# A fifth token tile for the gathered path of a product-key expert layer, and one tile fewer in the third dense chunk

## The reference

```python
q = (x @ Wq).reshape(b, t, H, 2, DK)                    # H = 4 heads
s1, i1 = top_k(sim1, 8); s2, i2 = top_k(sim2, 8)        # of 128 keys each
final_scores, pk_idx = top_k(s1[..., :, None] + s2[..., None, :], 8)
w_down = e_down[final_indices]; w_up = e_up[final_indices]
hidden = silu(einsum('btd,bthkd->bthk', x, w_down)) * relu(final_scores)
out = einsum('bthk,bthkd->btd', hidden, w_up)
x = x + tanh(g_ffn[3]) * out
```

## Time and profile before

| | us |
|---|---|
| median of 3 runs (1953.71 to 1954.48) | 1954.18 |
| the profiled execution's own time | 1956.58 |
| its span, first to last instruction | 1954.8 |
| busy: PE 1430.2, DVE 1471.8, ACT 903.4, POOL 485.4 | |
| `retrieve_phase`, from its first load | about 705 |
| chunk 0, chunk 1, chunk 2 of the dense path | 213.2, 217.3, 195.3 |

### The profile page before, as it was taken

The page is one execution under the profiler, slowest core; times in us unless marked ns, Lnnn a source line. Parts: engine busy times, 40 slices in busy tenths (PEclk is TensorE's granted clock), DMA queues, the critical chain, the costliest instruction groups (busy, mean ns, idle before and its releaser), DMA issues. The chain is left out here.

```text
span 1954.8 us, 24549 instructions
## 1 busy us (share of the span) xinstructions
PE 1430.2 (73%) x6624; PEld 1049.0 (54%) x6624; DVE 1471.8 (75%) x3100; ACT 903.4 (46%) x1768; POOL 485.4 (25%) x483
## 2 busy tenths in 40 slices
PE   4899048868999407444562488079999899999998
PEld 2455014436777203233431387068888778877776
DVE  7999479972555598699669599696777778886775
ACT  3464446643333141154321122138888688873343
POOL 0000012220000041423104022402455355545530
PEclk8999579988999755665695699599999999999999
DMA  4010400001000210145200100304666676667753
GB/s 161 22 33 1 177 6 1 0 18 47 1 0 0 92 50 1 43 156 171 71 1 10 49 22 22 104 9 145 182 202 206 180 209 204 204 195 218 215 173 113
DMA packets 82130, 181.51 MB, mean 93 GB/s; under 512 B 13832, under 2 KB 23176, under 8 KB 81168
## 3 DMA queue, kind: packets, MB, share of 16 engines
q0 software_dynamic: 27120, 91.25, 16.5%
q1 hardware_dynamic: 54944, 89.56, 13.9%
HBM read 165.04 MB, written 15.73 MB: 92 GB/s over the span
## 5 line engine op out<-in xcount | busy, mean ns | idle before, releaser
L2117 POOL DMA_INDIRECT L3f_gd<-rows,idx x128 | 151.2, 1181 | 309.2 <-DVE L3f_gd L2336 301.3
L2182 PE MATMUL L3f_o_ps<-L3f_euh,L3f_ath 128*128 128x512 f32 x384 | 158.4, 413 | 15.3 <-DVE L3f_atl L2317 14.6
L2170 PE MATMUL L3f_h_ps<-L3f_xh,L3f_edh 128*128 128x512 f32 x384 | 151.0, 393 | 7.9 <-DVE L3f_xl L2322 7.9
L2155 PE MATMUL L3f_g_ps<-L3f_oh 128*128 128x128 f32 x768 | 106.5, 283 | 62.1 <-DVE L3f_oh L2305 62.1
L2182 PE MATMUL L3f_o_ps<-L3f_euh,L3f_atl 128*128 128x512 f32 x384 | 151.1, 394 | 0.0
L2182 PE MATMUL L3f_o_ps<-L3f_eul,L3f_ath 128*128 128x512 f32 x384 | 150.8, 393 | 0.0
L2170 PE MATMUL L3f_h_ps<-L3f_xl,L3f_edh 128*128 128x512 f32 x384 | 150.6, 392 | 0.0
L2170 PE MATMUL L3f_h_ps<-L3f_xh,L3f_edl 128*128 128x512 f32 x384 | 150.3, 391 | 0.0
L2117 POOL DMA_INDIRECT L3f_gu<-in_L_ffn_e_up,idx x128 | 128.0, 1000 | 67.5 <-issue 36.4
L2155 PEld LDWEIGHTS L3f_g_ps<-L3f_oh 128*128 128x128 f32 x768 | 100.4, 195 | 73.4 <-issue 68.2
L2313 DVE TENSOR_TENSOR L3f_at<-L3f_at,L3f_G 128x512 f32<-128x512 f32 x96 | 66.2, 690 | 96.1 <-ACT L3f_at L2219 81.7
(11 more groups left out here) (509 smaller groups left out, 3681.7 us busy)
## 6 DMA issues: line engine op xcount, KB each, us to landing
L3f_eu<-in_L_ffn_e_up SPq DMA_DIRECT2D x96, 256.0 KB
L3f_ed<-in_L_ffn_e_down SPq DMA_DIRECT2D x96, 256.0 KB
L2x_ed<-in_L_ffn_e_down POOLq DMA_DIRECT2D x32, 256.0 KB, 3.8
rows<-L2x_eo POOLq DMA_DIRECT2D x32, 256.0 KB, 2.6
ternary_wgu<-in_L_ffn_w_gate_upT SPq DMA_DIRECT2D x4, 1408.0 KB, 8.8
X<-in_x SPq DMA_DIRECT2D x4, 1024.0 KB, 10.3
L0x_V<-in_ctxT SPq DMA_DIRECT2D x8, 512.0 KB, 3.9
L1f_C<-in_ctx SPq DMA_DIRECT2D x2, 2048.0 KB
```

The costliest lines, as they stand in the source:

```text
L2117: pool.indirect_dma_start(buf[j % ND][:, :], None, table, bass.IndirectOffsetOnAxis(ap=idx[:, j:j + 1], axis=0)).then_inc(sem[j % ND], 16)
L2155: last = pe.matmul(g_ps[h][:, g, :], lhsT=oh2[h][:, g, :], rhs=oh1[h][:, g, :], start=True, stop=True)
L2170: last = pe.matmul(h_ps[h][:, :], lhsT=w[h][:, c, :], rhs=x[:, c, :], start=(c == 0 and m == 0), stop=(c == DC - 1 and m == 2))
L2182: last = pe.matmul(o_ps[a][:, :], lhsT=w[h][:, a * P:(a + 1) * P], rhs=x[h][:, :], start=False, stop=False)
```

## The change

A constant `NG` = 5 replaces the 4 gathered tiles; `TG` becomes 11, `NU` 160, and the chunks have `tiles` = 4, 4 and 3 tiles. In chunks 0 and 1 a turn takes four pairs; in chunk 2 it takes three, three, three and two, in turns of four, 44 in all. The matmuls of `hidden` in chunk 2 have 384 columns, and `add_up`, `begin` and `end` go over three tiles; `silu`, `weight`, `high`, `low` take 384 columns there. There are 88 groups to build (`NO`) and no longer 96, so building ends with turn 27, `one_hot` with turn 26. To find room, `far` is gone: `one_hot` writes its intermediate into `oh1` and works in place, and `io` and `zero` use the memory of `ident` and `identb`. The final stores are of five and of three tiles.

```diff
+NG = 5
...
-    TG, S, SG, LAG, ND = NT - 4, 32, 8, 12, 6
-    NU = 4 * S
+    TG, S, SG, LAG, ND = NT - NG, 32, 8, 12, 6
+    NU = NG * S
+    tiles = [min(4, TG - 4 * q) for q in range(NQ)]
...
+    NO = TG * P // (4 * GR)
...
-            c = 3
+            c = 4 if q < NQ - 1 else 3 - (k % 4 == 3)
             pairs_in[q, k] = range(u, min(u + c, NU + LAG))
...
-        def hidden(n):
+        def hidden(n, q):
+            cols = tiles[q] * P
...
-                        last = pe.matmul(h_ps[h][:, :], lhsT=w[h][:, c, :], rhs=x[:, c, :],
+                        last = pe.matmul(h_ps[h][:, 0:cols], lhsT=w[h][:, c, :], rhs=x[:, c, 0:cols],
...
-                for a in range(4):
+                for a in range(tiles[q]):
                     for w, x in ((ath, euh), (ath, eul), (atl, euh)):
...
         def one_hot(n, h):
...
-            if done:
-                act.wait_ge(oh1_ready, done)
             for g in range(GR):
-                act.activation(far[:, g, :], io[:, :], ACT.Abs, scale=-1.0, bias=first[:, 0, n * GR + g:n * GR + g + 1]).then_inc(far_ready, 1)
+                act.activation(oh1[h][:, g, :], io[:, :], ACT.Abs, scale=-1.0, bias=first[:, 0, n * GR + g:n * GR + g + 1]).then_inc(far_ready, 1)
...
-            build = q < NQ - 2 or q == NQ - 2 and k < NP - 1
-            if q < NQ - 1:
+            held, build = n + EB < NO, n + EB + 2 < NO
+            if held:
                 keep(n + EB, q + 1, k, 0)
...
-        for t in range(4):
-            dve.tensor_scalar(xs[:, t, :], X[:, TG + t, :], stat[:, t:t + 1], stat[:, 4 + t:5 + t],
+        for t in range(NG):
+            dve.tensor_scalar(xs[:, t, :], X[:, TG + t, :], stat[:, 0, t:t + 1], stat[:, 1, t:t + 1],
```

More of the change, by code:

```diff
@@ L1825, in route_phase @@
     E1 = A["L3_ffn_e_down"].shape[0]
-    NQ, TG = 3, NT - 4
+    NQ, TG = 3, NT - NG
     tg = R["tg"]
@@ L1890, in _, with pair @@
         pe.wait_ge(k_in, 32)
-        def pair(i, regroup):
+        def pair(i, *regroup):
             for h in range(2):
@@ L1915, in _ @@
         with pe.Fori(0, TG // 2) as i:
-            pair(i, True)
+            pair(i, True, True)
         for i in range(TG // 2, NP):
-            pair(i, False)
+            pair(i, 2 * i < TG, False)
     @block.scalar
@@ L2183, in add_up, with end @@
                 last.then_inc(used, 1)
-        def end():
-            for a in range(4):
+        def end(q):
+            for a in range(tiles[q]):
                 last = pe.matmul(o_ps[a][:, :], lhsT=zero[:, :], rhs=zero[:, 0:1].to_broadcast([P, D]), start=False, stop=True)
@@ L2195, in _ @@
             pe.wait_ge(xl_ready, DC * (q + 1))
-            hidden(q * EB)
+            hidden(q * EB, q)
             begin(q)
[L2198 to L2202, removed]
+            add_up(q * EB, q, q < NQ - 1, q > 0)
+            built = min(NP, max(1, (NO - (q + 1) * EB) // 2))
+            if built > 1:
+                with pe.Fori(1, built) as k:
+                    hidden(q * EB + 2 * k, q)
+                    add_up(q * EB + 2 * k, q, True)
+            if built < NP:
+                with pe.Fori(built, NP) as k:
+                    hidden(q * EB + 2 * k, q)
+                    add_up(q * EB + 2 * k, q, False)
+            end(q)
     @block.scalar
@@ L2363, in turn @@
                 down_low(n + 2, 0)
-            low(n, 0)
+            low(n, 0, cols)
             up_low(n + 1, 1)
@@ L2367, in turn @@
             gathered(js[:1])
-            low(n + 1, 1)
+            low(n + 1, 1, cols)
             if more:
@@ L2393, in _ @@
         for q in range(NQ):
-            dve.wait_ge(G_ready, (q + 1) * EB + 2)
+            dve.wait_ge(G_ready, min((q + 1) * EB, NO) + 2)
             for k in range(NP):
-                turn(q, k, q < NQ - 2 or q == NQ - 2 and k < NP - 1, q < NQ - 1 or k < NP - 1)
+                turn(q, k, (q + 1) * EB + 2 * k + 2 < NO, q < NQ - 1 or k < NP - 1)
             if q < NQ - 1:
```

57 lines of the change are left out of this document (29 added, 28 removed).

## The result

| | before | after |
|---|---|---|
| median, us | 1953.95 (1952.1 to 1954.48, 4 runs) | 1979.87 (1978.92 to 1984.16, 4 runs) |
| profiled execution, its span | 1956.58, 1954.8 | 1978.92, 1977.1 |
| chunk 0 | 213.1 | 231.4 |
| chunk 1 | 217.3 | 234.9 |
| chunk 2 | 195.4 | 183.4 |

The change makes the kernel slower: the ratio is 1.0136, with an interval of 1.0119 to 1.0152. Chunks 0 and 1 give away 35.9 us, chunk 2 takes back 12.0, start and tail 1.7; together that is the 22.3 us between the two spans.

What follows compares the result with a forecast made beforehand. Chunks 0 and 1 stood where PE's floor meets the `ed` load loop, chunk 2 on the `eu` loop. -19 + 27.6 - 1 + 0.5 + 1.3 = +9.4 us gave 1963.6 us; likeliest case 1958 to 1980, full range 1930 to 1984.

Steps and rivals of the forecast that it cites:

- T = 9.38 + L: Chunks 0 and 1: turn time T in us, L the second `ed` load's latency from issue to copy; at least 12.69.
- A fourth pair a turn: Chunks 0 and 1: extra gathers lengthen the awaited `ed` load to L = 4.6, +1.1 us a turn; +27.6 us in all.
- Narrower chunk: Chunk 2: 384-column matmuls cut PE's work, but the `eu` loop holds back part of the gain; -19 us.
- The clock rival: Chunk 2: PE's idle time lowers its clock, 2.7 us each fall, +16 us in six turns, 1980 us; chance 0.05.
- The first rival: Chunks 0 and 1: extra gathers do not delay the `ed` load, L near 3.5; about 1934 us, faster; chance 0.32.
- Both loops lengthen: Chunks 0 and 1: the `eu` load is delayed too, ACT waits twice a turn, T about 15; 1998 us; chance 0.05.
- The break-even: Chunks 0 and 1: the `ed` load's latency L below which the change gains, put at 3.85 us.
- cancel: Whole kernel: L near 3.9 and chunk 2 as forecast offset each other, within 4 us of 1954; chance 0.13.
- DVE's cover: Chunks 0 and 1: DVE's 1.37 us idle ahead of the next `weight` takes the fourth pair's 1.36 us for nothing.
- Fewer groups: After turn 27: building ends earlier, so PE and ACT have less work, turns about 12.7 us; -1 us.
- Chunk 1 to chunk 2: At this change of chunk DVE passes straight from its last pair to `split_x`, so the fourth pair shows; +1.3 us.
- Prelude: Before the chunks: one more `xs`; +0.5 us.

Runs made afterwards that it cites:

- e9: Changed kernel, but the fourth pair's `gd` gather (ahead of the `ed` load) fetches 128 of 512 columns, the `gu` gather whole; 1945.55 us (1 run).
- e10: Changed kernel, but the fourth pair's `gu` gather (behind the `ed` load) fetches 128 of 512 columns, the `gd` gather whole; 1968.66 us (1 run).
- e4: Changed kernel with the fourth pair moved on DVE from the turn's end to behind the second pair; 1982.48 us (4 runs), ratio 1.0154.
- e2: Changed kernel with three pairs in every turn and only 128 of its 160 pairs, the last tile's gathered part left out; 1935.43 us (1 run).
- e5: Changed kernel with two buffers each for `ed` and `eu`, and `ND` = 5; 1913.59 us (4 runs), ratio 0.9804 to the kernel before.
- e3: Changed kernel, but both gathers at the fourth place of a turn fetch 128 of 512 columns; 1947.23 us.
- e1: Kernel before, with its 4 gathered tiles, taking four pairs a turn in chunks 0 and 1 and nothing else of the change; 1989.7 us (1 run).
- e12: Changed kernel, but POOL holds back the fourth pair's two gathers until ACT has copied the next turn's second `ed` load; 1999.77 us (4 runs), ratio 1.024.
- e8: Changed kernel with two buffers for `ed`, one for `eu`, and `ND` = 5; 1929.16 us (1 run).

## Why the prediction was right or wrong

The direction was right and the loop named was the one that binds; the size was too small, 9.4 us where the profiled executions show 22.3 (medians: 25.9).

- **The form T = 9.38 + L**: right, in all 17 undisturbed turns.
- **"A fourth pair a turn", L = 4.6: the first term that failed.** The bound above was the `eu` load's 5.21, and the discount, "another load had been issued shortly ahead of it, so I stay under it", had no price in the trace: there was such a load, an `ed` issued 1.9 us ahead at 1802.37, but nothing read there said what it cost. L measured 4.98 and 5.19, so +1.4 and +1.8 a turn and not +1.1: 26 us in 17 turns, where the term had 19. e9, e10 and e4 show what should have been asked of that row: not how many gathers are near the load, but whether one was issued just before it. The `eu` load had one 1.2 us ahead, and so has the new one, at 0.5.
- **"Narrower chunk", -19: the second term that failed**; it came to -12.0. The working took 9 us off ten turns with gathers and 8 off the five behind them; the runs show 5 and 6. It did not ask what the `ed` buffer's round takes when `silu` no longer sets it: 6.3 to 6.6 us a block, 12.9 a turn where it shows; ACT's waits for `ed` stood in the trace of before, 8.9 us beside the 10.8 for `eu`. And it put the clock at nothing. e2, without the fourth pair, gets 15.0 us, so 4 of the missing 7 us are there without it; the other 3 are no more than single runs differ by. One reading of the working was off as well: the turns with gathers took not 11.8 us but 12.5 (turns 32 to 41 of before, 1754.48 to 1879.94), since 16 turns less five are 11 and not 11.7.
- **The clock rival** was given 0.05 and "in six turns it is +16". It came in part, beside the forecast: by the estimate above the lower level costs 6.3 us more in chunk 2 than before (8.0 against 1.7). The forecast said "in pieces too short for it"; single waits of up to 3.5 us for `atl`, 22.1 us in all, stood against that. The Trainium skill's warning (TensorE: Matmul & The Clock Gate, HAM oscillation), that DMA waits between bursts of matmuls send the clock down again and again, agrees with this trace, which has four falls in chunk 2 where before had one. That it is worth 6 us is estimated, and seen on the chain for one fall of 2.8 us; it was not tried alone. e5, with doubled buffers, has no fall in chunk 2, and e2 and e3, with single ones, have several.
- **The first rival** (no delay, 1934) fell by L. While the load was under way, POOL's queue moved 0.77 MB in turn 11 where it had moved 0.36. The Trainium skill's rule that each DMA engine goes round between the queue rows that have work (DMA: Bandwidth & Descriptors, Queues, rings and completion order) did not exempt the load, though it has a queue of its own. In what order the engines took the packets is not shown here. **Both loops lengthen** (1998) fell too: in chunk 0 ACT waits for no `eu` load between 1390 and 1530 us.
- **The break-even** was misread: by the forecast's own sum, which changes by 24 us for 1 us of L, +9.4 becomes 0 at L = 4.2 and not at 3.85. So "cancel" belonged at 4.2, and at 3.9 the sum has -7. L came out above either, so this changed nothing in the direction.
- **DVE's cover** of 1.37 us: right, and used up to the last tenth.
- **Fewer groups** (-1): turns 27 to 30 take 52.0 us, where they took 51.8; nothing. In e1, which builds on with four pairs, they take 57.3. **Chunk 1 to chunk 2** (+1.3): turn 31 to the end of `split_x` is 3.2 us longer. **Prelude** (+0.5) and **end** (0): -0.4 and -1.3.

Against the forecast chunks 0 and 1 are 2.4 and 4.9 us over 229 and 230, chunk 2 7.4 over 176, and the edges 2.2 below: 12.5, and with the rounding of the forecast's stages the 12.9 between 9.4 and 22.3.

## What to carry to other kernels

A buffer that is loaded again only when it has been used puts the load's whole latency into the loop; then "the DMA engines have room" says little, and what is issued just ahead of that load can be paid in each turn, as the gather 0.5 us ahead was here. Work out the round of each single buffer (issue, latency, copy, release) beside the engines' floors before filling idle time with other transfers, for the loops that bind now and for those that come next when one of them is shortened. Where such a round is within a few tenths of the floor, double the buffer first and judge the change then: here the same edit cost 26 us before and gained 22 after.

## What the runs showed that was not expected

- The order of issue counts more than the bytes near by: a 256 KB gather issued 0.5 us ahead of a 256 KB load lengthens it by 0.7 to 1.1 us against a gather of 64 KB; issued 0.9 us behind it, by nothing that the scatter of the turns lets one see (up to 0.4).
- The latency of the same load in the same place of the turn scatters from 3.51 to 6.13 us from turn to turn with whole gathers, and from 3.14 to 4.68 in e9.
- Gather issues on POOL (0.95 to 1.46 us and 0.3 of gap in e12) are a pace of their own: eight a turn are 10 us or more, and a wait put ahead of two of them moves all of them.
- A second buffer for `ed` alone, 2 KB in each partition, is worth some 50 us to the changed kernel (e8, one run with `ND` = 5, against its 1979.87), although `eu` stays single.
